# Expert scales applied behind the down product, with GpSimd adding up, in a fused graph layer and top-2 expert FFN

## The reference

```python
# x (10000, 128), adj (10000, 10000), experts E = 8, hidden H = 256, D = 128, all fp32
h = item_feat @ W_item.T + b_item
x = x + relu(adj @ h + layernorm(x) @ W_user.T + b_user)
xf = layernorm(x)
probs = softmax(xf @ gate_w + gate_b)
cw = probs where it is among the two largest of its row, else 0     # (10000, 8)
out = sum over e of cw[:, e] * (gelu(xf @ W1[e] + b1[e]) @ W2[e] + b2[e])
x = x + out
```

## Time and profile before

| | |
|---|---|
| median of 3 runs | 1698.33 us (1698.3 to 1698.5) |
| the profiled execution | 1698.34 us, its span 1696.5 us |
| TensorE, VectorE, ScalarE, GpSimd busy | 98%, 86%, 72%, 4% of the span |
| DMA | 423.73 MB, 250 GB/s over the span |

### The profile page before, as it was taken

How to read it: one execution, slowest core, us unless ns; L and a number is a source line. 1 busy time by engine, 2 the same in 40 slices (tenths; PEclk the granted TensorE clock), 3 DMA queues, 4 the chain that set the end, 5 groups by cost and what they waited for, 6 DMA issues and landing times.

```text
span 1696.5 us, 26827 instructions
## 1 busy us (share of the span) xinstructions
PE 1668.4 (98%) x7485; PEld 1354.0 (80%) x7485; DVE 1464.3 (86%) x2285; ACT 1230.0 (72%) x1596; POOL 68.4 (4%) x63
## 2 busy tenths in 40 slices
PE   7999999999999999999999999999999999999997
PEld 6878888888888888887878787888888888888864
DVE  5988989898888888888889898989898989898864
ACT  4778777777777677777777777767777777777764
POOL 1000000000000000000000000000000000000000
PEclk9999999999999999999999999999999999999999
DMA  9998777787877787777778787777777777777700
GB/s 358 331 334 286 246 265 249 254 252 261 250 256 254 254 252 259 250 257 248 254 240 268 247 265 254 255 251 252 260 249 266 249 254 254 258 251 258 253 24 13
DMA packets 124639, 423.73 MB, mean 250 GB/s; under 512 B 14262, under 2 KB 19895, under 8 KB 124619
## 3 DMA queue, kind: packets, MB, share of 16 engines
q1 hardware_dynamic: 120456, 415.41, 74.7%
q10 hardware_dynamic: 3314, 5.71, 0.9%
q0 software_dynamic: 848, 2.36, 0.4%
HBM read 418.31 MB, written 5.12 MB: 250 GB/s over the span
## 4 chain that ended last, share of the span: by engine, by line
PE 95%; DVE 2%; DMA 1%; ACT 1%; issue 0%; SPq 0%; ACTq 0%; DVEq 0%
PE acc L760 21%; PE acc L762 21%; PE acc L761 21%; PE ps_z L833 4%; PE ps_z L834 4%; PE ps_z L835 4%; PE ps_y L792 4%; PE ps_y L786 3%; PE ps_y L788 3%; PE ps_y L787 3%; PE ps_w L843 2%; PE acc L778 1%; PE ps_x L768 1%; PE ps_g L810 1%; DMA raw<-in_adj_main 1%; DVE gs_lo L680 1%
## 5 line engine op out<-in xcount | busy, mean ns | idle before, releaser
L543 DVE TENSOR_TENSOR a_lo<-raw,a_hi 128x1000 fp32r<-128x1000 f32 (+1 forms) x800 | 930.2, 1184 | 130.7 <-ACT a_hi L391 128.6
L391 ACT ACTIVATE a_hi<-raw 128x1000 fp32r<-128x1000 f32 (+1 forms) x800 | 800.3, 1025 | 213.4 <-PE acc L762 198.3
L760 PE MATMUL acc<-a_hi,h_hi 128*128 128x500 f32 x1580 | 644.6, 408 | 4.4 <-DVE a_lo L543 3.5
L762 PE MATMUL acc<-a_hi,h_lo 128*128 128x500 f32 x1580 | 614.5, 389 | 0.0
L761 PE MATMUL acc<-a_lo,h_hi 128*128 128x500 f32 x1580 | 613.3, 388 | 0.0
L760 PEld LDWEIGHTS acc<-a_hi,h_hi 128*128 128x128 f32 x1580 | 297.2, 188 | 73.5 <-issue 18.7
L761 PEld LDWEIGHTS acc<-a_lo,h_hi 128*128 128x128 f32 x1580 | 297.8, 188 | 67.6 <-issue 12.8
L762 PEld LDWEIGHTS acc<-a_hi,h_lo 128*128 128x128 f32 x1580 | 297.2, 188 | 60.3
L456 ACT ACTIVATE g_sb<-ps_z,b_sb 128x500 f32<-128x500 f32 x320 | 199.1, 673 | 96.0 <-DVE gs_lo L680 89.7
L680 DVE TENSOR_TENSOR gs_lo<-g_sb,gs_hi 128x500 fp32r<-128x500 f32 x240 | 151.9, 675 | 40.5 <-PE ps_y L788 39.3
L671 DVE TENSOR_TENSOR g_sb<-ps_w,g_sb 128x500 f32<-128x500 f32 x240 | 151.2, 672 | 7.5 <-ACT g_sb L456 7.5
(11 more groups left out here) (121 smaller groups left out, 1058.5 us busy)
## 6 DMA issues: line engine op xcount, KB each, us to landing
raw<-in_adj_main SPq DMA_DIRECT2D x780, 500.0 KB, 4.6
xr_sb<-in_xR SPq DMA_DIRECT2D x20, 250.0 KB
x_sb<-in_xT SPq DMA_DIRECT2D x20, 250.0 KB, 3.7
out<-r_sb ACTq DMA_DIRECT2D x20, 250.0 KB, 5.1
...
```

Source lines behind the costliest of these rows:

```text
L391: nc.scalar.activation(a_hi[q][0:rows, 0:cols], raw[s][0:rows, 0:cols], ACT.Copy).then_inc(hi_ready, 1)
L543: nc.vector.tensor_tensor(a_lo[s][0:rows, 0:cols], raw[s][0:rows, 0:cols], val(a_hi[q][0:rows, 0:cols]), ALU.subtract).then_inc(lo_ready, 1)
L760: nc.tensor.matmul(acc[:, 0:T], w_hi, m_hi, start=(k == 0), stop=False)
L762: last = nc.tensor.matmul(acc[:, 0:T], w_lo, m_hi, start=False, stop=(k == KT))
```

## The change

The scales no longer go through TensorE. ScalarE copies the turned `cw` to SBUF and stores it to DRAM (`scales`, 8 rows of 500); SP loads each row back into all 128 partitions (`spread_sb`, 4 buffers). Gelu's output is split unscaled, so expert e's down product is unscaled too and gets a bank of its own (`ps_y`, two in turn; four for the last block). Behind it VectorE computes (y + b2) * scale in one instruction (`t_sb`), and GpSimd adds the eight results to x1 in `o_sb`. All eight experts have split down products, `g_sb`, `g_hi` and `g_lo` are doubled, experts start at 14, 19, ... 49, and the down product comes 8 positions later.

The last 16 items are laid three times into the partitions 0, 32 and 64 of one tile, so that high by high, low by high and high by low are one product. The token statistics and the normalisation read PSUM directly, `xn_hi` and `xn_lo` are made from PSUM, and the copies `xt` and `x1_kept` are gone, as are `pick`, `b2_hi` and `b2_lo`. The cut diff:

```diff
-STARTS = (27, 31, 35, 39, 44, 49, 54, 59)
-NSPLIT = 6
-DOWN = [8 if e < NSPLIT else 6 for e in range(E)]
+STARTS = tuple(range(14, 14 + 5 * E, 5))
+DOWNS = tuple(p + 8 for p in STARTS)
+SCALES = (32, 34, 37, 40, 45, 50, 55, 60)
+ADDS = tuple(p + 1 for p in SCALES)
+LAST_SCALES = (37, 38, 42, 43, 47, 52, 57, 60)
+SPREADS = 4
+S_SPREAD = (34, 34, 34, 35, 40, 45, 49, 54)
 W_SPLIT = 16
-AHEAD = 2
-A_RELU, A_TOKEN, A_NORM, A_EXP, A_SPLIT, A_SPREAD, A_STORE, A_KEEP, A_USER, A_FFN, A_SCALED = 2, 5, 12, 17, 25, 26, 31, 37, 38, 4, 6
-V_X1, V_STATS, V_NORM, V_LO, V_FINISH, V_USTATS, V_UNORM, V_FFN, V_SCALED = 2, 7, 9, 25, 29, 12, 34, 4, 7
-V_LOGITS, V_PROB, V_COMPARE, V_RANK, V_WEIGHT, V_SPREAD = 16, 18, 20, 21, 22, 26
+A_RELU, A_NORM, A_XN, A_EXP, A_SPREAD, A_SEND, A_STORE, A_USER, A_FFN, A_SCALED = 2, 11, 13, 17, 26, 27, 30, 38, 4, 6
+V_X1, V_STATS, V_NORM, V_LO, V_USTATS, V_UNORM, V_SCALED = 2, 5, 8, 12, 13, 34, 7
+V_LOGITS, V_PROB, V_COMPARE, V_RANK, V_WEIGHT = 16, 18, 20, 21, 22
+P_TAIL, P_USER = 6, 14
...
+        spread_sb = [sb(f"spread_sb{s}", [P, T]) for s in range(SPREADS)]
+        t_sb = [sb(f"t_sb{s}", [P, T]) for s in range(2)]
+        scales = nc.dram_tensor("scales", (E, T), fp32).ap()
...
+        ps_y = [bank(f"ps_y{s}") for s in range(2)]
+        last_y = [ps_y[0], ps_y[1], acc, ps_x]
...
+            def spread(i, p):
+                for e in range(E):
+                    if p != S_SPREAD[e]:
+                        continue
+                    if e == 0:
+                        sp.wait_ge(cw_stored, i * 16)
+                    since(sp, scaled, expert(i, e) - (SPREADS - 1))
+                    sp.dma_start(spread_sb[e % SPREADS][:, :],
+                                 scales[e].partition_broadcast(P)).then_inc(spread_landed[e % SPREADS], 16)
...
+            def add(i, p):
+                for e in range(E):
+                    if p != ADDS[e]:
+                        continue
+                    pool.wait_ge(scaled, expert(i, e) + 1)
+                    if e == 0:
+                        since(pool, stored, i * 16 - 16)
+                        pool.wait_ge(x1_ready, i)
+                    else:
+                        pool.wait_ge(added, expert(i, e))
+                    nc.gpsimd.tensor_tensor(o_sb[:, :], x1_sb[:, :] if e == 0 else o_sb[:, :], t_sb[e % 2][:, :],
+                                            ALU.add).then_inc(added, 1)
...
-                if p == A_TOKEN:
-                    act.wait_ge(t_turned, i)
-                    nc.scalar.activation(xt_sb[0:TQ, :], ps_v[0:TQ, :], ACT.Copy).then_inc(xt_ready, 1)
                 if p == A_NORM:
                     act.wait_ge(t_back, i)
+                    since(act, z_done, (i - 1) * (E * HH))
+                    nc.scalar.activation(xn_hi[:, :], ps_x[:, 0:T], ACT.Copy).then_inc(xn_hi_ready, 1)
+                if p == A_XN:
+                    act.wait_ge(xn_lo_ready, i)
                     nc.scalar.activation(xn_sb[:, :], ps_x[:, 0:T], ACT.Copy).then_inc(xn_ready, 1)
-                if p == A_SPLIT:
-                    act.wait_ge(xn_ready, i)
-                    if not (isinstance(i, int) and i == 1):
-                        act.wait_ge(z_done, i * (E * HH) - E * HH)
-                    nc.scalar.activation(xn_hi[:, :], xn_sb[:, :], ACT.Copy).then_inc(xn_hi_ready, 1)
                 if p == A_EXP:
                     act.wait_ge(shift_ready, i)
                     nc.scalar.activation(exp_sb[:, :], shift_sb[:, :], ACT.Exp).then_inc(exp_ready, 1)
-                if p == A_KEEP:
-                    if not (isinstance(i, int) and i == 1):
-                        act.wait_ge(out_ready, i - 1)
-                        act.wait_ge(stored, i * 16 - 16)
-                    act.wait_ge(x1_ready, i)
-                    nc.scalar.activation(x1_kept[:, :], x1_sb[:, :], ACT.Copy).then_inc(kept_ready, 1)
                 if p == A_SPREAD:
                     act.wait_ge(cwT_done, i)
-                    nc.scalar.activation(cw_parts[0:E, :], ps_g[0:E, 0:T], ACT.Copy).then_inc(cw_hi_ready, 1)
+                    since(act, cw_stored, i * 16 - 16)
+                    nc.scalar.activation(cwT_sb[:, :], ps_g[0:E, 0:T], ACT.Copy).then_inc(cwT_ready, 1)
+                if p == A_SEND:
+                    act.wait_ge(cwT_ready, i)
+                    since(act, scaled, expert(i, 0))
+                    act.dma_start(scales, cwT_sb[:, :]).then_inc(cw_stored, 16)
...
                     e = STARTS.index(p - A_FFN)
-                    if not (isinstance(i, int) and i == 1 and e == 0):
-                        if 0 < e <= NSPLIT:
-                            act.wait_ge(gs_lo_ready, i * (NSPLIT * HH) + HH * (e - NSPLIT))
-                        else:
-                            act.wait_ge(gs_ready, i * (E * HH) + HH * (e - E))
+                    since(act, down_done, expert(i, e) - 1)
                     for j in range(HH):
                         act.wait_ge(z_done, i * (E * HH) + (HH * (e - E) + j + 1))
-                        nc.scalar.activation(g_sb[j][:, :], ps_z[j][:, 0:T], ACT.Gelu,
+                        nc.scalar.activation(g_sb[e % 2][j][:, :], ps_z[j][:, 0:T], ACT.Gelu,
                                              bias=b1_sb[:, e * HH + j:e * HH + j + 1]).then_inc(gelu_ready, 1)
-                if p - A_SCALED in STARTS[:NSPLIT]:
+                if p - A_SCALED in STARTS:
                     e = STARTS.index(p - A_SCALED)
-                    if not (isinstance(i, int) and i == 1 and e < 2):
-                        act.wait_ge(down_done, i * E + (e - E - 1))
                     for j in range(HH):
-                        act.wait_ge(gs_ready, i * (E * HH) + (HH * (e - E) + j + 1))
-                        nc.scalar.activation(gs_hi[e % 2][j][:, :], g_sb[j][:, :], ACT.Copy).then_inc(gs_hi_ready, 1)
+                        act.wait_ge(gelu_ready, i * (E * HH) + (HH * (e - E) + j + 1))
+                        nc.scalar.activation(g_hi[e % 2][j][:, :], g_sb[e % 2][j][:, :], ACT.Copy).then_inc(g_hi_ready, 1)
...
-                rows, cols = (P, CT * T) if p < NC else (KREM, T)
-                nc.vector.tensor_tensor(a_lo[s][0:rows, 0:cols], raw[s][0:rows, 0:cols],
-                                        val(a_hi[q][0:rows, 0:cols]), ALU.subtract).then_inc(lo_ready, 1)
+                whole, high = raw[s][:, :], a_hi[q][:, :]
+                low = a_lo[s][:, :]
+                if p == NC:
+                    whole, high = (t[LO_ROW:LO_ROW + KREM, 0:T] for t in (raw[s], a_hi[q]))
+                    low = high
+                nc.vector.tensor_tensor(low, whole, val(high), ALU.subtract).then_inc(lo_ready, 1)
...
-                    dve.wait_ge(xt_ready, i)
-                    moments(1, xt_sb[0:TQ, :], t_stats, t_moments, t_var, i)
+                    dve.wait_ge(t_turned, i)
+                    moments(1, ps_v[0:TQ, :], t_stats, t_moments, t_var, i)
                 if p == V_NORM:
                     dve.wait_ge(t_rstd, i)
-                    normalise(1, xt_sb[0:TQ, :], xt_sb[0:TQ, :], t_normed)
+                    normalise(1, xt_sb[0:TQ, :], ps_v[0:TQ, :], t_normed)
                 if p == V_LO:
                     dve.wait_ge(xn_hi_ready, i)
-                    nc.vector.tensor_tensor(xn_lo[:, :], xn_sb[:, :], val(xn_hi[:, :]), ALU.subtract).then_inc(xn_lo_ready, 1)
+                    nc.vector.tensor_tensor(xn_lo[:, :], ps_x[:, 0:T], val(xn_hi[:, :]), ALU.subtract).then_inc(xn_lo_ready, 1)
...
-                if p - V_FFN in STARTS:
-                    e = STARTS.index(p - V_FFN)
-                    dve.wait_ge(spread_done, i * E + (e + 1 - E))
-                    if e > NSPLIT:
-                        dve.wait_ge(down_done, i * E + (e - E))
+                if p - V_SCALED in STARTS:
+                    e = STARTS.index(p - V_SCALED)
                     for j in range(HH):
-                        dve.wait_ge(gelu_ready, i * (E * HH) + (HH * (e - E) + j + 1))
-                        scaled = g_sb[j] if e < NSPLIT else gs_sb[j]
-                        nc.vector.tensor_tensor(scaled[:, :], ps_w[:, 0:T], g_sb[j][:, :],
-                                                ALU.mult).then_inc(gs_ready, 1)
-                if p - V_SCALED in STARTS[:NSPLIT]:
-                    e = STARTS.index(p - V_SCALED)
-                    if not (isinstance(i, int) and i == 1 and e == 0):
-                        dve.wait_ge(down_done, i * E + (e - E))
-                    for j in range(HH):
-                        dve.wait_ge(gs_hi_ready, i * (NSPLIT * HH) + (HH * (e - NSPLIT) + j + 1))
-                        nc.vector.tensor_tensor(gs_lo[j][:, :], g_sb[j][:, :], val(gs_hi[e % 2][j][:, :]),
-                                                ALU.subtract).then_inc(gs_lo_ready, 1)
-            def finish(i):
-                dve.wait_ge(down_done, i * E - E)
-                dve.wait_ge(kept_ready, i - 1)
```

(124 more changed lines are left out.)

142 lines of the change are left out of this document (58 added, 84 removed).

## The result

The changed kernel takes 1680.61 us (1680.22 to 1681.53) against 1698.41 (1698.3 to 1698.54) for the kernel before, timed side by side: ratio 0.9896, 95% interval 0.9879 to 0.9913. It is 1.0% faster. The forecast was 1626, range 1611 to 1664: the sign was right, the size wrong by 55 us.

A forecast was written before the change was run, and what follows sets the result against it. The prediction took TensorE's queued work to bound the kernel, 81.67 us a pass. From 1698.3 us, -56.9 (passes), +5.7 (stalls), -20 (end) and -1.5 (start) gave 1625.6, range 1611 to 1664.

The forecast's parts named there:

- Term 1: TensorE in the 19 passes after the first: a pass falls from 81.67 to 78.31 us, -56.9 us in all.
- term 2: TensorE stalls in the passes from GpSimd's adds delaying VectorE: 0.3 us a pass, +5.7 us, bounds 0 and 38.
- Rival 1: In the passes, the adds make VectorE the joint bound: a pass of 80.5 us, 1662 in all; chance 0.16.
- Rival 2: In the passes, VectorE alone sets the pace, say 83.5 us a pass: 1719 in all, slower; chance 0.09.
- Rival 3: The spread of the scales comes late and VectorE stands at position 32: 1668 us; chance 0.06.
- rival 4: The end does not shrink (clock, adds in a chain): 1646 us; chance 0.06.
- Term 3: The end, after the last adjacency matmul: 68.0 us becomes 48, -20 us, bounds -24 and -8.
- Term 4: The start: half a MB of pick no longer loaded while DMA is full, -1.5 us, bounds 0 and -4.

The follow-up runs named there:

- both causes gone: Changed kernel with each GpSimd add cut to 4 of 500 columns, and ScalarE's high part at 13, exp at 19, products unmoved: 1629.16 us.
- the block alone: Changed kernel with each GpSimd add cut to 4 of its 500 columns, the rest of the sum left out: 1645.41 us.
- the waits alone: Changed kernel with ScalarE's high part at 13 (was 11) and exp at 19 (was 17), TensorE's products left where they were: 1661.48 us.

## Why the prediction was wrong

**Term 1** was right as work: with both causes gone the passes take 1492.9 against the 1479.7 worked out, and the fp32r matmuls cancelled (7485 matmuls before, 7325 after: the 160 fp32 ones are gone).

**VectorE's load** came out near: 74.88 against 75.8; an add costs it 0.75 us (6.0 / 8) where I took 0.9, and works 1.24 (the one near the end, at 1670.53) where I took 1.2. Both had been picked between wide bounds, so that they fit is in part luck. The splits grew little, but the other sign that the forecast had named for being wrong, adds of 2 us, is there: 2098 ns, 1.24 of it work and the rest waiting.

**The step that failed is the conversion of this load into TensorE's standing, term 2** (+5.7, bounds 0 and 38; measured 59.5). I had written that a deficit of 1 to 2 us in positions 0 to 22 is covered by a lead of 5.4 less 1.7. That lead is not there at position 12. In the pass shown above VectorE itself stands behind ScalarE's wait of 4.32 us, and the adjacency product catches up with the splits:

```profile
837.72 1.20 DVE L600 TENSOR_TENSOR a_lo<-raw,a_hi 128x1000 fp32r<-128x1000 f32 x1 [1.81 <-ACT a_hi L458]
```

```profile
838.98 0.50 PE L792 MATMUL acc<-a_hi,h_hi 128*128 128x500 f32 x1 [0.19 <-DVE a_lo L600]
```

ScalarE waits at 11 for the transposes and the eighth up product at 9, and exp at 17 hangs on a gate product at 14. I had named the first as "two steps as before" and costed it at nothing. The kernel before did wait there, two steps behind the transposes, and TensorE had no idle time:

```profile
ACT xn_sb L421 <- PE ps_x L768: 70.0, 20, 3.7
```

But the diff also moves the wait for `z_done` from position 25 to 11, and with the new STARTS it puts one more product, 1.36 us, into the wait (85.5 us in all, the longest 4.9); and I spent the same lead twice, on this wait and on the adds. The runs show it: the block alone is 35 us, the waits alone 19, and together 51, so each keeps nearly all of its worth when the other is gone. The last 13.2 us of the passes stay open.

**Rival 1**, the adds make VectorE the joint bound, is nearest: it gave a pass of 80.5 and 1662; TensorE stood 3.1 a pass instead of 2.2, and 1680.6 is beyond it. It had a chance of 0.16, and no case of mine joined it with ScalarE's waits. Rival 2 (VectorE alone, 1719) did not come: VectorE idles 6 us a pass. Rival 3 did not come: VectorE waited 8.6 us in all for the spread, and less traffic gains 5. Nor did rival 4: the end shrank by 18.7.

**Term 3**: the end gave -18.7 for -20. The first up stands at 1642.22, 13 us behind the last adjacency work (11 forecast), the last at 1667.75:

```profile
1642.22 0.48 PE L861 MATMUL ps_z<-xn_hi,w_hi 128*128 128x500 f32 x1
...
1667.75 0.39 PE L861 MATMUL ps_z<-xn_hi,w_hi 128*128 128x500 f32 x1
...
1676.28 0.37 ACTq L521 DMA_DIRECT2D out<-o_sb  x1
```

From the third up to the sixth the cadence was the forecast 2.7 to 2.8, then 4.0 and 4.2 where the adds had begun. With four-column adds they are 2.7 and the end is 44.3 instead of 51.0; with all adds on VectorE they are 3.5 and 3.9 and the end is 47.6, so the adds cost time here on either engine. **Term 4**: -2.3 for -1.5; no run separates its parts.

Open: what the last 13 us in the passes of the slack version with four-column adds are, and why the gate's difference came late when the eighth up product was moved up (ScalarE waited 49.3 us for it there). Neither was tried further.
